# Expert blocks added straight into the output tensor, instead of into an accumulator that is copied

## The reference

```
x = x + self_attention(layernorm(x))            # 16 heads, window of 64
x = x + cross_attention(layernorm(x), context)  # 16 heads, 375 context rows, bias by bucketed distance
x = x + experts(layernorm(x))                   # 8 experts of width 512, the 2 likeliest of each token

experts(x):  probs  = softmax(x @ router_w.T), kept for the top 2, made to sum to 1
             h      = silu(x @ gate_w[e] + gate_b[e]) * (x @ up_w[e] + up_b[e])
             result = sum over e of probs[e] * (h @ down_w[e] + down_b[e])
```

## Time and profile before

| | us |
|---|---|
| median of 3 timed runs | 1335.68 |
| the profiled execution's own time | 1333.42 |
| its span, first to last instruction | 1331.8 |
| TensorE busy (matmuls) | 1227.9 (92%) |
| VectorE, GpSimd, ScalarE busy | 870.9, 859.0, 728.9 |
| first block ends, by the barrier | 946.2 |
| last copy issued, first to last start | 1317.9 to 1319.8 |

### The profile page before, as it was taken

How to read it: one execution, slowest core, us unless ns; L and a number is a source line. 1 busy time by engine, 2 the same in 40 slices (tenths; PEclk the granted TensorE clock), 3 DMA queues, 4 the chain that set the end, 5 groups by cost and what they waited for, 6 DMA issues and landing times. The chain is left out here.

```text
span 1331.8 us, 40106 instructions
## 1 busy us (share of the span) xinstructions
PE 1227.9 (92%) x13828; PEld 1090.0 (82%) x13829; DVE 870.9 (65%) x3949; ACT 728.9 (55%) x1827; POOL 859.0 (65%) x1597
## 2 busy tenths in 40 slices
PE   5399999999999999999999999995399999999993
PEld 3388888888888888888888888884399999999993
DVE  2266888788878887887778877786244444444441
ACT  2256666666666666666666666663244444444440
POOL 4267787887878787878787878765244444444431
PEclk8889999999999999999999999997699999999997
DMA  8910100111011101110011001101476222222224
GB/s 164 158 62 24 43 27 28 35 45 29 27 35 35 40 27 31 35 43 28 27 38 43 28 28 31 28 13 40 157 201 152 50 49 48 48 48 47 46 39 126
DMA packets 47316, 73.20 MB, mean 55 GB/s; under 512 B 6832, under 2 KB 34032, under 8 KB 47088
## 3 DMA queue, kind: packets, MB, share of 16 engines
q1 hardware_dynamic: 31408, 45.74, 13.0%
q0 software_dynamic: 15744, 25.31, 9.8%
HBM read 46.90 MB, written 27.80 MB: 56 GB/s over the span
## 5 line engine op out<-in xcount | busy, mean ns | idle before, releaser
L470 POOL TENSOR_SCALAR arena<-arena,mC 112x375 f32<-112x375 f32 x512 | 299.5, 598 | 136.9 <-DVE mC L857 136.7
L857 DVE CUSTOM_DVE_ANT_0 arena<-bank_S,arena 112x375 f32<-112x375 f32 x512 | 264.9, 543 | 112.6 <-PE bank_S L599 64.8
L1099 POOL DMA_INDIRECT acc<-y,xb x64 | 119.4, 1866 | 206.5 <-DVE y L1243 182.9
L476 POOL TENSOR_SCALAR arena<-arena,mF 112x112 f32<-112x112 f32 x512 | 177.6, 367 | 22.8 <-DVE mF L845 21.2
L741 ACT ACTIVATE pTC<-bank_Q 126x336 f32<-126x336 f32 x286 | 128.6, 450 | 45.7 <-PE bank_Q L609 44.5
L707 ACT ACTIVATE arena<-bank_B 128x224 f32<-128x224 f32 (+5 forms) x229 | 87.4, 382 | 110.0 <-PE bank_B L530 35.0
L707 ACT ACTIVATE arena<-bank_A 128x224 f32<-128x224 f32 (+3 forms) x219 | 82.2, 376 | 112.0 <-PE bank_A L622 28.1
L1230 DVE SCALAR_TENSOR_TENSOR hT<-bankU,gub,gate 128x128 f32<-128x128 f32 x256 | 72.1, 344 | 107.4 <-PE bankU L1139 95.1
L609 PE MATMUL bank_Q<-ident,arena 112*126 112x112 f32 x858 | 130.8, 261 | 0.5 <-ACT pTC L741 0.5
L1139 PE MATMUL bankG<-xbT,gwb 128*128 128x128 f32 x1024 | 126.6, 277 | 1.0 <-ACT gwb L1186 1.0
L1139 PE MATMUL bankU<-xbT,uwb 128*128 128x128 f32 x1024 | 124.8, 275 | 0.0
(11 more groups left out here) (206 smaller groups left out, 2926.8 us busy)
## 6 DMA issues: line engine op xcount, KB each, us to landing
arena<-in_l_ctxT SPq DMA_DIRECT2D x32, 378.0 KB, 3.6
xb<-xs POOLq DMA_DIRECT2D x64, 129.0 KB, 3.5
arena<-in_L_ffn_gate_w SPq DMA_DIRECT2D x8, 512.0 KB, 4.4
arena<-in_L_ffn_up_w SPq DMA_DIRECT2D x8, 512.0 KB, 5.4
arena<-in_L_ffn_down_w SPq DMA_DIRECT2D x8, 512.0 KB, 3.7
arena<-in_x SPq DMA_DIRECT2D x32, 112.0 KB, 2.1
acc<-arena SPq DMA_DIRECT2D x32, 112.0 KB, 1.9
out<-acc SPq DMA_DIRECT2D x4, 896.0 KB, 9.1
```

The lines of the kernel that those rows point to most:

```text
L470: pool.tensor_scalar(z[n % NZ][:, 0:T], z[n % NZ][:, 0:T], -1.0, mC[:, n:n + 1], ALU.mult, ALU.add).then_inc(s_u, 1)
L476: m = pool.tensor_scalar(sF[r][:, j, :], sF[r][:, j, :], -1.0, mF[:, r, j:j + 1], ALU.mult, ALU.add)
L857: dve.tensor_tensor_reduce(out=z[n % NZ][:, 0:T], in0=bank[f"S{r}"][0:S, 0:T], in1=nbias[:, n, :], scale=1.0, scalar=3.0e38, op0=ALU.add, ...
L1099: pool.indirect_dma_start(out=acc[:, :], out_offset=bass.IndirectOffsetOnAxis(ap=xb[x][:, D + 1:D + 2].bitcast(I32), axis=0), in_=y2[x % 2 ...
```

## The change

`acc` is gone. The x2 rows are stored into the output tensor and the expert blocks are added into it; the output tensor now has N + 128 rows, so that the padding rows have somewhere to go, and the host drops these 128 rows after the run. The 4 copies, their semaphore and the wait for them are gone. Beside that, the waits in the first block whose value is a constant, 23 lines, call `wait_ge` in place of `need`. `need` skips a wait that its engine has had already; `wait_ge` always issues it. Most of these lines run once. Those inside helpers that run several times for batch 0 are shown.

```diff
-    acc = nc.dram_tensor("acc", (N + P, D), F32, kind="Internal").ap()
...
                         elif step == "st":
                             drained_wait(sp, "woc", b)
-                            sp.dma_start(acc[b * S:(b + 1) * S, :], x2[b % 2][:, :]).then_inc(s_st[b % 2], 16)
+                            sp.dma_start(out[b * S:(b + 1) * S, :], x2[b % 2][:, :]).then_inc(s_st[b % 2], 16)
...
                     def probs_back(n, b, B_, F_):
                         if b == 0:
-                            need(pe, s_pool, 2)
+                            pe.wait_ge(s_pool, 2)
...
                         if b == 0 and g == 0:
-                            need(pe, s_pool, 2)
+                            pe.wait_ge(s_pool, 2)
...
                     def slots(b, B_, F_):
                         if b == 0:
-                            need(pe, s_pool, 2)
+                            pe.wait_ge(s_pool, 2)
...
                         if b == 0 and step in ("k0", "k1", "v0", "v1"):
-                            need(pe, s_wkv, 1)
+                            pe.wait_ge(s_wkv, 1)
                         B_, F_ = fill_wait(pe, step, b), fill_sem(step, b)
                         if place[step, b] in (("A", 0), ("B", 0)):
-                            need(pe, s_fc, 1)
+                            pe.wait_ge(s_fc, 1)
...
                     def cross_probs(n, b):
                         B_ = filled_wait(act, f"p{n}", b)
                         if b == 0:
-                            need(act, s_skw, 32)
+                            act.wait_ge(s_skw, 32)
...
                             elif b == 0:
-                                need(act, s_pool, 2)
+                                act.wait_ge(s_pool, 2)
...
                         filled_wait(dve, f"S{g}", b)
                         if b == 0:
-                            need(dve, s_nb, 16)
+                            dve.wait_ge(s_nb, 16)
...
                     sp.wait_ge(s_add, 16 * NBLK)
-                    NO = 4
-                    for n in range(NO):
-                        sp.dma_start(out.rearrange("b s d -> (b s) d")[n * N // NO:(n + 1) * N // NO, :],
-                                     acc[n * N // NO:(n + 1) * N // NO, :]).then_inc(s_out, 16)
-                    sp.wait_ge(s_out, 16 * NO)
...
                         pool.indirect_dma_start(
-                            out=acc[:, :], out_offset=bass.IndirectOffsetOnAxis(ap=xb[x][:, D + 1:D + 2].bitcast(I32), axis=0),
+                            out=out[:, :], out_offset=bass.IndirectOffsetOnAxis(ap=xb[x][:, D + 1:D + 2].bitcast(I32), axis=0),
                             in_=y2[x % 2][:, :], in_offset=None, compute_op=ALU.add).then_inc(s_add, 16)
...
-    out = nc.dram_tensor("out", arrays["x"].shape, F32, kind="ExternalOutput").ap()
+    B, S, D = arrays["x"].shape
+    out = nc.dram_tensor("out", (B * S + P, D), F32, kind="ExternalOutput").ap()
     decoder_layer(nc, aps, out)
...
-    return r.results[0]["out"]
+    return r.results[0]["out"][0:B * S, :].reshape(B, S, D)
```

More of the change, by code:

```diff
@@ L401, in _ @@
                     load_c(1)
-                    need(sp, s_fc, 1)
+                    sp.wait_ge(s_fc, 1)
                     for i, (o, w) in enumerate(((0, U // 2), (U // 2, U - U // 2))):
@@ L406, in _ @@
                                      fbias[i].rearrange("h (o u) -> h o u", o=1).to_broadcast([H, S, w])).then_inc(s_skw, 16)
-                    need(sp, s_skw, 32)
+                    sp.wait_ge(s_skw, 32)
                     skewed = bass.AP(skew.tensor, S - 1, [[H * U - 1, S], [U, H], [1, T]])
@@ L411, in _ @@
                         load_package(sp, 0, half)
-                    need(sp, s_pad0, 1)
+                    sp.wait_ge(s_pad0, 1)
                     sp.dma_start(xs[E * R:E * R + P, :], pad[:, :]).then_inc(s_spare, 16)
@@ L424, in _ @@
                             drained_wait(sp, "woc", b)
-                            sp.dma_start(acc[b * S:(b + 1) * S, :], x2[b % 2][:, :]).then_inc(s_st[b % 2], 16)
-                    need(sp, s_pad, 16 * E)
-                    need(sp, s_spare, 16)
+                            sp.dma_start(out[b * S:(b + 1) * S, :], x2[b % 2][:, :]).then_inc(s_st[b % 2], 16)
+                    sp.wait_ge(s_pad, 16 * E)
+                    sp.wait_ge(s_spare, 16)
                     for q in range(2):
@@ L449, in _ @@
                     pool.memset(ones[:, :], 1.0).then_inc(s_pool, 1)
-                    need(pool, s_const, 16 * NCONST)
+                    pool.wait_ge(s_const, 16 * NCONST)
                     def deviation(i, b):
@@ L497, in _ @@
                             scatter(b)
-                    need(pool, s_padi, 1)
+                    pool.wait_ge(s_padi, 1)
                     for e in range(E):
@@ L506, in _ @@
                 def _(pe):
-                    need(pe, s_const, 16 * NCONST)
+                    pe.wait_ge(s_const, 16 * NCONST)
                     pe.matmul(bank["A"][0:H, 0:U // 2], relb[:, :], one_hot[:, 0:U // 2], start=True, stop=True)
@@ L511, in _ @@
                       .then_inc(s_fb, 1)
-                    need(pe, s_pool, 1)
+                    pe.wait_ge(s_pool, 1)
                     def transposes(dst, src, m, then):
@@ L638, in _ @@
                             late = True
-                            need(pe, s_late, 16 * NLATE)
+                            pe.wait_ge(s_late, 16 * NLATE)
                         if b == 0 and step in ("k0", "k1", "v0", "v1"):
-                            need(pe, s_wkv, 1)
+                            pe.wait_ge(s_wkv, 1)
                         B_, F_ = fill_wait(pe, step, b), fill_sem(step, b)
                         if place[step, b] in (("A", 0), ("B", 0)):
-                            need(pe, s_fc, 1)
+                            pe.wait_ge(s_fc, 1)
                         if step == "xT":
@@ L754, in _ @@
                             if b == 0:
-                                need(act, s_pool, 1)
+                                act.wait_ge(s_pool, 1)
                             drain("v", b, vS[:, :, 0:DH], lambda t: v3(t, H, DH, S))
@@ L898, in set_up @@
                     def set_up():
-                        need(dve, s_const, 16 * NCONST)
-                        need(dve, s_fb, 1)
+                        dve.wait_ge(s_const, 16 * NCONST)
+                        dve.wait_ge(s_fb, 1)
                         dve.tensor_scalar(fbias[0], bank["A"][0:H, 0:U // 2], -1.0, None, ALU.mult)
@@ L907, in set_up @@
                         dve.tensor_copy(pad[:, D + 1:D + 2].bitcast(I32), rowf[:, :]).then_inc(s_pad0, 1)
-                        need(dve, s_pad0, 1)
+                        dve.wait_ge(s_pad0, 1)
                         link(dve.tensor_scalar(rowf[:, :], rowf[:, :], float(-N), None, ALU.add))
@@ L913, in split_weights @@
                     def split_weights():
-                        need(dve, s_late, 16 * NLATE)
+                        dve.wait_ge(s_late, 16 * NLATE)
                         link(dve.tensor_copy(wkv[0][:, :, :], wkv_in[:, :, :]))
@@ L1059, in decoder_layer @@
             s_taken = sem("pool_waits_taken2")
-            s_out = sem("output_stored")
             def back(k):
```

## The result

The median is 1323.32 us (1322.44 to 1323.85, 4 runs), where the kernel before took 1335.77 (1335.61 to 1337.4, 4 runs, measured beside it). The ratio is 0.9902, with a 95% interval of 0.9886 to 0.9917. The prediction was 1324.0, with 1321.2 to 1327.0 as its range. The profiled execution took 1323.08 us with a span of 1321.4 us; before it was 1333.42 with 1331.8. The profiles are 10.3 us apart, the medians 12.5; the other 2 us are taken up further down.

The account below looks back on a forecast made before the run. TensorE bounds the expert stage at 5.53 us a block; at the end the copy runs with nothing beside it. 11.8 us gone and 0.1 added make -11.7: 1335.68 - 11.7 = 1324.0 us, range 1321.2 to 1327.0.

Parts of the forecast that it names:

- The copy goes, 13.5 us of it on the path: Program end: four copy issues (2.8 us) and SyncE's 10.7 us wait, with nothing beside them, disappear: 13.5 us.
- The estimate from the Trainium skill's "DMA: Bandwidth & Descriptors", "Anatomy of one DMA": End copy: 2.0 us plus 3.67 MB at 436 GB/s, so only 10.4 us would go; the trace's 13.5 was used.
- GpSimd's drain is late next and takes back 1.7 us: Second block's end: the drain, hidden under the copy, ends at 1319.5 and holds the barrier; gain 11.8 us, not 13.5.
- 0.3 us from the drain's end to the barrier instruction: Second block's end: gap behind GpSimd's drain, from the first block's 945.8 to 946.1, counted into the new end 1320.0.
- The adds and stores into the output cost nothing: 32 x2 stores and 64 scatter-adds move to the output tensor, number, size and order unchanged: zero cost taken.
- The slower adds as a rival: Expert stage: adds landing slower in the output become the bound past 4.8 us; at 5.2 us, 1352.5; chance 0.05.
- The repeated waits, 0.1 us taken, 1.7 kept as a bound: First batch: 52 added waits on TensorE, ScalarE and VectorE, mostly hidden, 0.1 us; 1.7 us if end to end.
- The first expert block at the same time to within 0.5 us: Sign in the changed profile: expert stage starts as before; 1 to 2 us later would mean the repeated waits cost.
- Profile to median: Whole run: the 11.7 us found in the profile is subtracted from the timed median 1335.68, giving 1324.0.

Follow-up runs that it names:

- e1: The kernel before without the four copies and their wait, so the output is never written: 1320.58 us, ratio 0.9903 to the kernel before.
- e3: The changed kernel with GpSimd also waiting for the last add's landing before its drain: 1323.62 us, ratio 0.9930 to the kernel before.
- e4: The changed kernel with a 384-column GpSimd memset between an add's landing and the next add: 1325.05 us, ratio 0.9939 to the kernel before.
- e5: The changed kernel with a 1152-column GpSimd memset between an add's landing and the next add: 1359.07 us, ratio 1.0189 to the kernel before.
- e2: The kernel before with only the change's repeated waits, accumulator and copy kept: 1332.38 us, ratio 0.9992 to the kernel before.
- e8: The changed kernel without an edit, measured again on another chip: 1321.99 us, ratio 0.9913 to the kernel before.
- e6: The changed kernel with GpSimd's 8 padding scatters replaced by plain DMAs, 4 from SyncE and 4 from ScalarE: 1311.97 us, ratio 0.9834 to the kernel before.
- e7: The changed kernel with 8 more GpSimd padding scatters, into a spare tensor ahead of the real ones: 1332.47 us, ratio 0.9990 to the kernel before.

## Why the prediction was right, step by step

- *The copy goes, 13.5 us of it on the path.* Right: e1, with nothing else changed, has the whole gain. The estimate from the Trainium skill's "DMA: Bandwidth & Descriptors", "Anatomy of one DMA" (10.4 us, which with the drain late next would leave 8.7), was too low; the interval of e1's gain begins at 11. That section gives its fit for DMAs issued from GpSimd, and this copy is issued by SyncE, so the page did not price this case; the prediction did not say so.
- *GpSimd's drain is late next and takes back 1.7 us.* Right in what is late next and in its size; why the drain takes that long the prediction left open, and the guess that I made before e3 was wrong. In the tail the gain is 11.9 us, against 11.8. One piece was mis-sized: I added 0.3 us from the drain's end to the barrier instruction, taken from the first block; in the tail that is under 0.1 us.
- *The adds and stores into the output cost nothing.* Right: landing 4.2 us in both, and 343.8 us for the 64 blocks in both. The prediction had only rows of other transfers for this; e1 beside the changed kernel is the test.
- *The slower adds as a rival.* That they would decide past the slack and at about what price was right (e4, e5 bracket the point between 0.5 and 1.1 us an add); what did not happen is the slower landing.
- *The repeated waits, 0.1 us taken, 1.7 kept as a bound.* Right side: e2 finds no cost. I had priced all 52 as instructions; 34 more are recorded.
- *The first expert block at the same time to within 0.5 us.* Wrong: it comes 1.5 us later in the profile of the changed kernel. I would have read it as the cost of the waits. It is not: near 911 us the changed kernel was 1.1 us ahead (its first store of x2 goes out at 107.8, before at 108.7), and it lost 2.6 us between there and the barrier, where TensorE's clock fell earlier. That is told in the last section. It makes the profiles' difference smaller than the tail's gain: 11.9 - 1.5 = 10.4.
- *Profile to median.* I subtracted the difference of the profiled execution from the median: forecast 1324.0, measured 1323.32. The error of 0.7 us is smaller than the spread of 1.4 us between runs of the changed kernel, and that it is so small is partly luck. The changed kernel's profiled execution (1323.08) is as fast as its median (1323.32), the one before (1333.42) is 2.4 us faster than its median (1335.77). That makes 12.5 us of medians out of 10.3 us of profiles. What made the timed runs before slower is not shown; on the two chips of the experiments the kernel before ran in 1333.72 and 1333.37 us, and on the second of them the changed kernel (e8) gained 11.4.

## What to carry to other kernels

When a transfer at the very end is taken away, the end moves to what the barrier waits for next, and its row is already in the trace, hidden under the transfer: look at every engine's DRAIN, not only at who waited for the transfer. GpSimd, which issues the indirect DMAs here, paid 3.8 to 6.6 us in its drain at the end of both blocks. So look at every barrier, not only at the last, whether its last such DMA can come earlier or be made by another queue, as in e6; it pays only until something else ends last. And do not let GpSimd wait for its last landing when another engine does so anyway (e3: 2.4 us in the tail). Who adds in a chain, each waiting for the one before, should compare landing plus hand-over with the period of the bound engine before moving the target: here 0.57 us were left, 0.5 more per add was hidden but for the tail, and 1.1 was not.

## What the runs showed of the hardware that I had not expected

**GpSimd's drain costs 3.8 us with nothing outstanding** (3821 ns in e3, the DMA landed before), and 5.3 to 6.6 us behind plain scatters. SyncE's takes 7 ns, and GpSimd's own at the program's start 171 ns. So the microseconds belong to GpSimd after its DMAs or its work in these blocks; that the indirect DMAs cause them is not shown, as no run ends a block of GpSimd without them.

**The moment at which TensorE's clock falls at the end of the first block goes with 2.5 us.** Busy time of 905 to 930 us, first in the kernel before, then in the changed one; the third column from the right is the granted clock:
```profile
905.00:930.00 25.00, 11.77 (x138) 9.00 (x136) 16.83 (x106) 7.44 (x21) 10.71 (x17) 0.75 0.12 34
```
```profile
905.00:930.00 25.00, 12.60 (x125) 9.44 (x121) 14.60 (x95) 6.67 (x19) 9.53 (x16) 0.65 0.08 24
```
As the pipeline of the attention stage runs empty, TensorE is busy about half of the time (11.77 and 12.60 of 25 us), and from some moment in this stretch it is granted half of its speed (1.2 instead of 2.4 GHz); from 930 us to the barrier the granted clock is 0.50 in both. In the changed kernel that came earlier relative to the work. The table counts from one and the same matmul near the end of the stage, the 11,100th; all profiles record 13828 matmuls.

| profile | clock 905 to 930 us | clock falls, us behind the matmul | matmul to barrier, us |
|---|---|---|---|
| e4 | 0.81 | 7.9 | 34.4 |
| e1 | 0.75 | 7.5 | 34.4 |
| before | 0.75 | 5.7 | 34.4 |
| e8, the changed kernel again | 0.73 | 4.9 | 34.4 |
| e2 | 0.70 | 4.7 | 34.4 |
| e5 | 0.71 | 3.7 | 34.9 |
| e3 | 0.68 | 2.6 | 35.4 |
| the changed kernel | 0.65 | 1.9 | 36.9 |

The order is without exception: where the clock fell 4.7 us or more behind this matmul nothing was lost, and where it fell earlier the loss was the larger the earlier it fell. e6 and e7 have other work behind the stage; from the same matmul to the block's last one they take 13.65 us, the kernel before 13.64. The same kernel stands in the table twice, with 36.9 and 34.4 us, so this is no effect of the change.

Behind the barrier there is a second such spread, which the experiments did not look for. In the ten profiles the clock rises again 11.4 to 14.9 us behind the barrier, and VectorE's first step on a block's result comes 19.4 to 21.2 us behind it, in the same order but for differences under 0.1 us; e8 is 0.2 us ahead of the kernel before at the barrier and 1.1 us behind it at this step.

So the profile of one execution is good to about 2.5 us here, and differences of that size must be read from the stage that they concern, or from medians. That the clock causes the losses is read from these orders; no run held the clock fixed.
